# Z products in the attention drain, constants loaded early, and a two-bank GELU in quarters

## The reference

```python
x = x + tanh(g_xattn[0]) * attention(layernorm(x), ctx)   # 32 heads, 8 kv heads, rmsnorm on q and k
t = layernorm(x)[:, perm]                                 # features permuted
t = gelu(einsum('bhd,hdm->bhm', t, up))                   # 16 heads of 32 -> 128
x = x + tanh(g_ffn[0]) * einsum('bhm,hmd->bhd', t, down)[:, unperm]
p, g, v = Wp @ layernorm(x), Wg @ ctx, Wt @ ctx           # per block of 128 channels
att = sum(p * g) per group of 16 channels
y = groupnorm(Wz @ (att * v)) * gn_w + gn_b + ctx
x = x + tanh(g_xattn[1]) * y
x = x + tanh(g_ffn[1]) * experts(layernorm(x))            # one of 8 experts for each token
```

## Time and profile before

| what | value |
|---|---|
| median of 3 runs | 853.31 us (850.31 to 854.73) |
| the profiled execution | 851.44 us |
| its span in the trace | 849.7 us |
| PE busy | 770.1 us (91%) |
| ACT, DVE, POOL busy | 489.3, 484.1, 338.5 us |
| mean granted TensorE clock | 0.956 of full speed |

### The profile page before, as it was taken

The page is one execution under the profiler, slowest core; times in us unless marked ns, Lnnn a source line. Parts: engine busy times, 40 slices in busy tenths (PEclk is TensorE's granted clock), DMA queues, the critical chain, the costliest instruction groups (busy, mean ns, idle before and its releaser), DMA issues. The chain is left out here.

```text
span 849.7 us, 13807 instructions
## 1 busy us (share of the span) xinstructions
PE 770.1 (91%) x3850; PEld 605.1 (71%) x3850; DVE 484.1 (57%) x885; ACT 489.3 (58%) x1840; POOL 338.5 (40%) x639
## 2 busy tenths in 40 slices
PE   5999958999999999999999999999988888678990
PEld 3888846888888887888887888888876333255760
DVE  4775304556556555565565655655666456646773
ACT  4543217776766765766666676676552655334760
POOL 0330014443443444344353453453232455125883
PEclk9999979999999999999999999999999898867995
DMA  8435641021021021012002003000021577513436
GB/s 293 146 123 159 186 132 62 15 74 63 14 73 65 14 74 64 13 33 103 13 28 98 24 12 111 25 12 14 1 100 49 182 254 307 192 50 125 148 128 218
DMA packets 46151, 80.66 MB, mean 95 GB/s; under 512 B 5128, under 2 KB 25608, under 8 KB 42640
## 3 DMA queue, kind: packets, MB, share of 16 engines
q1 hardware_dynamic: 43536, 71.66, 24.8%
q0 software_dynamic: 2560, 8.39, 3.0%
HBM read 55.40 MB, written 24.64 MB: 94 GB/s over the span
## 5 line engine op out<-in xcount | busy, mean ns | idle before, releaser
L552 ACT ACTIVATE p_sb<-p_sb,nmax 128x128 f32<-128x128 f32 x256 | 99.7, 391 | 132.0 <-DVE nmax L698 132.0
L626 POOL TENSOR_TENSOR v_lo<-v_raw,v_hi 128x128 fp32r<-128x128 f32 x64 | 29.6, 462 | 258.2 <-ACT v_hi L590 258.2
L721 DVE TENSOR_TENSOR pT_lo<-bank,pT_hi 128x512 fp32r<-128x512 f32 x64 | 44.2, 691 | 48.9 <-ACT pT_hi L565 48.9
L763 PEld LDWEIGHTS bank<-kT,qT_sb 128*128 128x128 f32 x512 | 66.9, 191 | 7.1 <-ACT qT_sb L560 1.8
L631 POOL TENSOR_TENSOR p_sb<-p_sb,rsum 128x512 f32<-128x512 f32 x64 | 66.6, 1041 | 6.6 <-DVE rsum L717 6.6
L763 PE MATMUL bank<-kT,qT_sb 128*128 128x128 f32 x512 | 67.6, 275 | 1.4 <-ACT qT_sb L560 1.4
L597 ACT ACTIVATE q_junk<-bank 128x128 f32<-128x128 f32 x256 | 66.1, 272 | 4.2 <-PE bank L775 4.2
L689 DVE TENSOR_TENSOR oT_lo<-bank,oT_hi 128x512 fp32r<-128x512 f32 x64 | 44.0, 688 | 36.3 <-ACT oT_hi L547 36.3
L547 ACT ACTIVATE oT_hi<-bank 128x512 fp32r<-128x512 f32 x64 | 38.1, 595 | 40.2 <-PE bank L814 35.8
L392 PE MATMUL bank<-w_hi,ctx_hi 128*128 128x512 f32 x128 | 53.8, 420 | 7.6 <-DVE ctx_lo L323 7.6
L727 DVE SCALAR_TENSOR_TENSOR x_sb<-bank,tgates,x_sb 128x512 f32<-128x512 f32 x64 | 48.0, 751 | 22.0 <-PE bank L803 22.0
(11 more groups left out here) (259 smaller groups left out, 2163.8 us busy)
## 6 DMA issues: line engine op xcount, KB each, us to landing
w_raw<-in_wq_l SPq DMA_DIRECT2D x8, 1024.0 KB, 5.5
w_raw<-in_wo_l SPq DMA_DIRECT2D x8, 1024.0 KB, 4.8
exp_w<-in_exp_w_l SPq DMA_DIRECT2D x8, 1024.0 KB, 11.9
kT_scr<-kT_st SPq DMA_DIRECT2D x16, 256.0 KB, 2.3
v_scr<-v_st SPq DMA_DIRECT2D x16, 256.0 KB, 2.6
sorted_x<-ctx_nat SPq DMA_DIRECT2D x1, 3840.0 KB, 11.9
hid<-sorted_x SPq DMA_DIRECT2D x15, 256.0 KB, 2.7
sorted_y<-ctx_nat SPq DMA_DIRECT2D x15, 256.0 KB, 2.1
```

What stands on the lines that cost most here:

```text
L552: last = act.activation(p_sb[:, b % 2, h * P:(h + 1) * P], p_sb[:, b % 2, h * P:(h + 1) * P], ACT.Exp, bias=nmax[:, b % 2, h:h + 1], accum ...
L763: last = pe.matmul(s_ps[:, h * P:(h + 1) * P], qT_sb[:, b % 2, h * P:(h + 1) * P], kT[:, b * P:(b + 1) * P], start=True, stop=True)
```

## The change

1. The ten constants are issued on SP right after the load of x, and `project_kv` no longer waits for them; PE waits for them at the start of `attention` (`s.mid_ld`).
2. `s.ctx_nat` has another place in the memory, is loaded at the start of the last head group, and Z products 0 to 3 stand in the drain of `attention` (`z01`, `z2`, `z3`), each with its copy on ACT. Z products 4 to 7 stand at the start of `middle`. SP's part of `attention` now ends with a wait for the last output projection.
3. The banks are allocated in pairs. GELU reads two banks in an activation, and the `up` products cycle through three pairs. The first half of the tokens is 4 packs of 512, the second half 8 packs of 256, so there are 12 packs. The second half is scattered and loaded back in two parts (`THIRDS`), with 12 scatters in all.
4. Expert weights 0 and 1 are issued behind the stores of `xT_scr`.
5. The order of the G products, of their copies and of the later statistics changes. In `experts` the statistics of the first half end before block 4 is updated.

```diff
+QTOK = 2 * P
+HALVES = ((0, HB), (HB, B))
+THIRDS = ((0, HB), (HB, HB + 2), (HB + 2, B))
...
+            if i >= lo + 2:
+                dve.wait_ge(bn_done, i - 1)
+                dve.bn_aggr(s.mv[:, i - 2, :], s.bn[:, i - 2, :]).then_inc(mv_done, 1)
+        layernorm_var(dve, s, mv_done, hi, slice(lo, hi)).then_inc(xval_done, 1)
 
 
 def negated_shift(dve, s, cols, rstd, shift):
@@ -103,9 +106,8 @@
                                     op0=ALU.mult, op1=ALU.mult)
 
 
-def layernorm_half_var(dve, s, step, count, c=None):
-
-    cols = slice(0, B) if c is None else slice(c * HB, (c + 1) * HB)
...
+            for dst, src in ((s.up[:, :, :], d.up), (s.down[:, :], d.down), (s.perm_col[:, :], d.perm_col),
+                             (s.wt[:, :], d.wt), (s.wzT[:, :], d.wzT), (s.wgT[:, :], d.wgT), (s.wpT[:, :], d.wpT),
+                             (s.group_mean[:, :], d.group_mean), (s.gn_w[:, :], d.gn_w), (s.gn_b[:, :], d.gn_b)):
+                sp.dma_start(dst, src).then_inc(s.mid_ld, 16)
...
-            for dst, src in ((s.up[:, :, :], d.up), (s.down[:, :], d.down), (s.perm_col[:, :], d.perm_col),
-                             (s.wt[:, :], d.wt), (s.wzT[:, :], d.wzT), (s.wgT[:, :], d.wgT), (s.wpT[:, :], d.wpT),
-                             (s.group_mean[:, :], d.group_mean), (s.gn_w[:, :], d.gn_w), (s.gn_b[:, :], d.gn_b)):
-                sp.dma_start(dst, src).then_inc(mid_ld, 16)
                 sp.wait_ge(first_ld[i], 48)
             sp.wait_ge(wo_ld, 16)
-            sp.wait_ge(mid_ld, 160)
 
...
+            sp.wait_ge(q_done, 8 * G - 8)
+            sp.wait_ge(o_done, 8 * G - 8)
+            sp.dma_start(s.ctx_nat[:, :, :], d.ctx).then_inc(s.ctx_nat_ld, 16)
+            sp.wait_ge(o_done, UNITS)
...
+            def copy_z(*bs):
+                for n in bs:
+                    act.wait_ge(s.z_done, n + 1)
+                    act.activation(s.z[:, n, :], z_ps[n][:, :], ACT.Copy).then_inc(s.z_copied[1], 1)
...
+            run(act, [(oT_split, -2), (exps, 0), (copy_z01, 0), (qT_copy, 1), (pT_split, -1), (copy_z2, -1), (copy_z3, -1),
+                      (v_split, 2), (q_stats, 2), (seed_ln2, -3), (copy_xT, -6)]
...
+                if after(u, b, g, B - 3):
+                    pe.wait_ge(s.z_copied[1], 2)
...
             def transpose_x(u, b, g, odd):
                 if after(u, b, g, HB - 1):
-                    pe.wait_ge(q_scaled, UNITS)
+                    pe.wait_ge(s.z_copied[1], HB)
                     pe.wait_ge(qT_copied, UNITS)
                     pe.wait_ge(masked, UNITS)
...
+            def z01(u, b, g, odd):
+                if after(u, b, g, B - 2):
+                    pe.wait_ge(s.ctx_nat_ld, 16)
+                    pe.wait_ge(q_scaled, u + 1)
+                    pe.wait_ge(acc_done, u - 2)
+                    z_product(0)
+                    z_product(1)
+
+            def z2(u, b, g, odd):
+                if after(u, b, g, B - 2):
+                    pe.wait_ge(s.z_copied[1], 1)
+                    z_product(2)
+
+            def z3(u, b, g, odd):
+                if after(u, b, g, B - 1):
+                    pe.wait_ge(q_scaled, UNITS)
+                    z_product(3)
...
+            run(pe, [(scores, 0), (q_proj, 2), (z01, 0), (q_transpose, 1), (p_transpose, -1), (z3, -1), (o_proj, -2),
+                     (z2, -1), (values, -1), (transpose_x, -5)])
...
+        ZA, ZD = (4, 5), (6, 7)
+
+        def pack(k):
+
+            if k < KT:
+                return k, slice(0, HALF)
+            q, jt = divmod(k - KT, KT)
+            return jt, slice(HALF + q * QTOK, HALF + (q + 1) * QTOK)
+
+        def hidden(k, j):
+
+            if k < KT:
+                return hid[:, 4 * (k % 2) + 2 * j:4 * (k % 2) + 2 * j + 2, :]
+            return hid[:, 2 * (k % 4):2 * (k % 4) + 2, :].rearrange("p a (c n) -> p (a c) n", n=QTOK)[:, 2 * j:2 * j + 2, :]
+
+        def hidden_free(k):
+
+            return 0 if k < 2 else k - 1 if k < KT else (k - KT) // 2 + 3 if k < 2 * KT else k - 3
...
-            sp.wait_ge(scattered[0], 16 * KT)
-            sp.dma_start(yU[:, :, 0:HALF], d.yT_scr[0].rearrange("(k p) n -> p k n", p=P)).then_inc(yU_ld[0], 16)
-            sp.wait_ge(s.o_done, UNITS)
             for e in (0, 1):
                 sp.dma_start(s.exp_w[:, e, :, :], d.exp_w[e]).then_inc(s.exp_ld, 16)
-            sp.wait_ge(scattered[1], 16 * KT)
-            for i in range(2):
-                sp.dma_start(yU[:, :, HALF + i * 2 * P:HALF + (i + 1) * 2 * P],
-                             d.yT_scr[1][:, i * 2 * P:(i + 1) * 2 * P].rearrange("(k p) n -> p k n", p=P))\
-                    .then_inc(yU_ld[1 + i], 16)
+            for c, (lo, hi) in enumerate(THIRDS):
+                sp.wait_ge(scattered[c], 16 * KT)
+                sp.dma_start(yU[:, :, lo * P:hi * P], d.yT_scr[c].rearrange("(k p) n -> p k n", p=P))\
+                    .then_inc(yU_ld[c], 16)
             for e in (2, 3, 6, 7):
                 sp.dma_start(s.exp_w[:, e, :, :], d.exp_w[e]).then_inc(s.exp_ld, 16)
             sp.wait_ge(y_done, B)
...
+            copy_z(4)
             act.wait_ge(xval_done, 2)
...
-            for n in range(PACKS):
-                reached(act, down_done, n - 1)
-                for i in range(HG):
-                    act.wait_ge(up_done, HG * n + i + 1)
-                    act.activation(hid[:, HG * (n % 2) + i, :], up_ps[i][:, :], ACT.Gelu).then_inc(gelu_done, 1)
+            for k in range(PACKS):
+                toks = pack(k)[1]
+                reached(act, down_done, hidden_free(k))
+                for j in range(2):
+                    act.wait_ge(up_done, 4 * k + 2 * j + 2)
+                    act.activation(hidden(k, j), up_ps[(2 * k + j) % 3][:, :, 0:toks.stop - toks.start], ACT.Gelu)\
+                        .then_inc(gelu_done, 1)
             act.preload_act_table_set(LN_EXP_SET)
-            for b in range(HB, B):
-                copy_z(b)
-            for b in range(3):
+            for b in range(5):
                 copy_g(b)
             seed3(0)
+            copy_g(5)
+            copy_g(6)
             normalise3(0)
-            copy_g(3)
-            copy_g(4)
+            copy_g(7)
             seed3(1)
-            for b in (5, 6, 7):
-                copy_g(b)
             normalise3(1)
+            seed3(2)
+            normalise3(2)
             act.wait_ge(col_step, 3)
...
-            for n in range(KT):
-                scatter(n)
             pool.wait_ge(ctx_nat_ld, 16)
             pool.wait_ge(col_step, 2)
-            scale_ctx(range(HB))
-            for n in range(KT, PACKS):
-                scatter(n)
-            scale_ctx(range(HB, HB + 2))
+            for jt in range(KT):
+                scatter(0, jt)
+            scale_ctx(range(2))
+            for jt in range(KT):
+                scatter(1, jt)
+            for jt in range(KT):
+                scatter(2, jt)
+            scale_ctx(range(2, HB))
             rstd3(0)
-            scale_ctx(range(HB + 2, B))
-            add_ctx(range(3))
+            scale_ctx(range(HB, B))
+            add_ctx(range(2))
             rstd3(1)
+            add_ctx(range(2, 3))
+            rstd3(2)
             add_ctx(range(3, B))
...
             copy_xT(4)
+            copy_z(6)
             copy_xT(6)
-            copy_z(2)
-            copy_z(3)
-            for b in range(HB):
-                z_stats(b)
-
+            for k in range(PACKS):
+                jt, toks = pack(k)
+                dve.wait_ge(down_done, k + 1)
+                dve.tensor_copy(yT[:, jt, toks], yT_ps[k % 2][:, 0:toks.stop - toks.start]).then_inc(yT_copied, 1)
+                if k < B - 1:
+                    z_stats(k + 1)
...
-                if b == HB + 2:
+                if b == HB:
                     shift(0)
...
-                if b == 1:
-                    shift(1)
+                if b == 2:
+                    shift(2)
...
+            for k in range(PACKS + 1):
+                if k < PACKS:
+                    jt, toks = pack(k)
+                    pe.wait_ge(gathered[(k >= KT) * KT + jt], 16)
                     for i in range(HG):
-                        reached(pe, gelu_done, HG * (n - 1) + i + 1)
+                        if i % 2 == 0:
+                            reached(pe, gelu_done, 2 * k + i // 2 - 2)
+                            if k == 0 and i == 2:
+                                pe.wait_ge(z_copied[0], 2)
                         rows = slice(FD * i, FD * (i + 1))
-                        pe.matmul(up_ps[i][:, :], s.up[rows, jt, :], xg[rows, jt, c * HALF:(c + 1) * HALF],
-                                  start=True, stop=True).then_inc(up_done, 1)
-                if n >= 1:
-
-                    k = n - 1
-                    kt = k % KT
-                    pe.wait_ge(gelu_done, HG * (k + 1))
-                    reached(pe, yT_copied, k - 1)
+                        pe.matmul(up_ps[(2 * k + i // 2) % 3][:, i % 2, 0:toks.stop - toks.start], s.up[rows, jt, :],
```

(35 more changed lines are left out.)

142 lines of the change are left out of this document (74 added, 68 removed).

## The result

The changed kernel takes 839.46 us (median of 4 runs, 838.90 to 841.75), the kernel before 853.21 in the same session: ratio 0.9848, 95% interval 0.9815 to 0.9880. A second session gave 838.18 and 0.9835 (0.9815 to 0.9854). It is faster, as forecast, but by 13.8 and 14.9 us and not by 22. The first session's median lies 5.0 above the top of the forecast (827 to 834.5) and 0.5 above the range that takes in the rivals (824 to 839); the second session's lies inside that range. The profiled execution is 839.96, its span 838.2.

What follows compares the result with a forecast made beforehand. PE bounds the long middle of `attention`; chains of waits bound the places changed. Terms -6.5, -2.0, -11.1 and -1.5 sum to -21.1 from 851.44, so 830.3, stated as 831; forecast 827 to 834.5, with rivals 824 to 839.

Steps and rivals of the forecast that it cites:

- the rivals: Cases inside 824 to 839: gathers pay for weights (0.13), small packs not cheap (0.10), seam or drain gives less (0.10).
- GELU stage: Packs from 663.0 taking 12.0 and 9.6 with some overlap: end at 683.4 against 687.4, -4.0 in all.
- the clock behind the seam: First q projection in `attention`: shorter PE idle leaves twelve products at full speed, -2.0, bounds 0 and -2.9.
- drain -1.2: End of `attention`: Z products in PE's waits keep the clock up, -1.2, bounds +0.3 and -1.2.
- the gathers' 1.0: Second four gathers in GELU, delayed by expert weights 0 and 1 issued in front: +1.0, bounds 0 and +4.
- Constants: Seam after `project_kv`: early constants let `attention` start at 114.35, -6.5; -4.4 if something else holds the barrier.
- What starts GELU: First `up` product: a gather's landing, not DVE's z copies, ends the wait, at 661.9, -1.5.
- some overlap at the seam between the sizes: In GELU, between large and small packs: overlap assumed when adding 12.0 and 9.6 from 663.0 to 683.4.
- Rival (b): GELU: small packs not cheap, clock stays low; second half at 2.1 a pack ends 7 later, 838; chance 0.10.
- The merged activation: ACT in GELU: estimated 0.92 for an activation of two banks, 0.52 for each one before.
- Behind GELU: Last GELU to `a_col`: about 30 us, 37.7 before; `a_col` at 713.0, -12.1 for all since the drain.
- `experts`: Last stage: first-half statistics no longer wait for updates 4 and 5, -1.5, bounds 0 and -1.8.

Runs made afterwards that it cites:

- constants_alone: The kernel before with only the ten constants issued behind the load of x and PE's wait for them at the start of `attention`; 846.86 us.
- before_again: The kernel before, unchanged, run once more for a second profile; 854.30 us, ratio 1.0005.
- after_again: The changed kernel, unchanged, run once more for a second profile; 838.18 us, ratio 0.9835.
- fewer_warm: The changed kernel with 7 in place of 10 unread PE products at the start of the last stage; 839.38 us.
- weights_mid: The changed kernel with expert weights 0 and 1 issued once all eight gathers have landed; 839.45 us.
- weights_late: The changed kernel with expert weights 0 and 1 issued behind the first load of yU, as in the kernel before; 839.85 us.
- weights_last: The changed kernel with expert weights 0 and 1 issued behind all loads of y; 841.96 us.
- all_of_them: The changed kernel with 8 packs of 512, 7 unread products, `xT_scr` stores ahead of SP's wait, weights 0 and 1 after all gathers; 841.39 us.
- big_early_last: The changed kernel with 8 packs of 512, 7 unread products, `xT_scr` stores ahead of SP's wait, weights 0 and 1 behind y's loads; 835.70 us.
- early_stores_mid: The changed kernel with `xT_scr` stores ahead of SP's wait and weights 0 and 1 issued after all gathers landed; 841.20 us.
- warm_before_up: The changed kernel with four more unread PE products ahead of the first `up` product; 840.76 us.

## Why the prediction was wrong

Two steps failed. The larger is the GELU stage, its start included: forecast to end at E+29.5, where it had ended at E+32.3, it ends at E+34.7. The other is the clock behind the seam, put in as a fixed -2.0. The sum in its own terms, from the two profiled executions, up to DVE's last operation (the spans, 849.7 and 838.2, differ by 11.5):

| part | forecast | measured |
|---|---|---|
| start of `attention` | -6.5 | -7.0 |
| `attention` to E (clock -2.0, drain -1.2) | -3.2 | -0.7 |
| E to `a_col`, with the gathers' 1.0 | -9.9 | -4.9 |
| `a_col` to the end | -1.5 | +1.2 |
| sum | -21.1 | -11.4 |

The medians give 13.8; part of the second and the last line differs from profile to profile of the same code, as shown below.

**Constants: right.** 6.96 in the profile; alone 5.9 in the median.

**Clock after the seam: wrong as a fixed term.** The failed step is "an idle of 2.53 in `project_kv` and the 2.92 in the drain left later products at full speed", read from one profile. The rows of 17 profiles with the same 2.3 idle show 0 to 15 slow products, so a short idle time doesn't decide it. Nor did the 2.92 hold as a premise: in constants_alone and before_again the same wait in the drain is followed by 6.8 us at the lower level (622.6 to 629.4 and 631.0 to 637.8). `attention` took 532.4 in the mean of these 17, and 534.3 and 536.0 in the two of the kernel before, so the 2.0 and 1.2 together are not far off as a mean (1.9 to 3.6), but this is partly luck: up to the drain the mean gain is 0.5 to 0.8 and not 2.0, and the drain brings the rest. This profile had drawn 13.

**Drain: right in kind, rather too small.** From the q transposes (632.43, now 626.18) to E 22.7 and 21.4, -1.3, and the clock 1.00. Against before_again and constants_alone (24.2) it is -2.8, beyond the bound of -1.2.

**What starts GELU: wrong by 2.3**, and with it "-1.5" turned into a loss. I had the first `up` 8.0 behind E. The first gather started at 5.0 and not 4.2 (the second store's landing), and took 5.3 and not 3.8. In the kernel before the first gather landed 3.6 after its start, ahead of the stores of blocks 4 to 7 (E+6.2 and E+6.8). Now these are issued at E+5.7 and E+6.6, beside it, and the weights add about 0.3 (E+9.9 without them). That the stores are what slows it is argued from this order; no run has them apart. With the stores ahead of SP's new wait the same product comes at E+6.6: the wait that the change put ahead of them costs 3.7 here.

**GELU stage: the largest miss.** Forecast end E+29.5, measured 34.7 (34.4 in after_again, 36.0 in fewer_warm, which has this code up to there). The 5.2 are, to 0.1, 2.3 from the late start, 1.0 since the first GELU waits 2.1 for products at low clock where I had 1.1, 1.5 from the small packs (11.1 for eight, at 1.34 each and a start, in place of 9.6), and 1.2 from "some overlap at the seam between the sizes" that isn't there; the first four packs, at 11.1, were 0.9 quicker than my 12.0. Nor was the kernel before a fixed point: its second profile ended GELU at 34.1 and not 32.3. Rival (b) had the right sign: small products cost PE more than half of large ones (0.71 and 0.64 for 256 columns, 1.14 and 1.07 for 512). The merged activation went as estimated: 1.02 each, 0.92 apart; those of the small packs, with 512 columns, start 0.49 apart. The difference, 0.43 for 512 more columns, is 0.84 ns a column. The Trainium skill ("ScalarE: Activation LUTs", section "What ACT_TABLE_LOAD costs", on the ACTIVATE instruction) has 0.833 ns, and the trace agrees.

**Gathers and weights: right in size, wrong in place.** The weights, issued at 654.51, hit gathers 2 and 3 most: these landed 9.5 and 10.5 after their start, gathers 4 to 7 took 8.0 down to 6.2. Gather 4 had landed at E+20.5, ahead of pack 4 at 23.5. With the weights out of the way GELU ended 1.3 to 1.6 earlier in weights_mid, but the low clock was shorter there too (E+9.7 to 16.5, in place of 9.3 to 19.6); in weights_late and weights_last it ended no earlier, with the stalled packs. So the cost to GELU lies between 0 and 1.6 (+1.0 forecast), and `a_col` shows none of it. The price behind GELU shows once GELU is quick: 4.9 on `a_col` between all_of_them and big_early_last, with the weights beside the first scatters. The Trainium skill ("DMA: Bandwidth & Descriptors", section "Issuing engines are not separate DMA queues") states that DMAs of different issuers run on the same engines and interleave; the landings agree (scatters 2 and 3 took 7.8 and 8.5 beside the weights, the last of the four at most 2.8 without them).

**Behind GELU: right.** 30.2, forecast 29.6.

**`experts`: mis-sized.** The statistics came 1.5 earlier, as reckoned, and PE's twenty records of unread products, 10.3 us, ended 1.2 after the block they cover was ready (724.15). I had read ACT's and DVE's rows only and never asked what stood in PE's queue. From the start of the stage to the first transpose 10.26 remained of 10.62, so 0.4 came of the 1.5; the barrier took 0.3 more. By PE's last product 0.2 was left of the gain, and from there to the end, where the output is gathered, it took 19.0 in place of 18.0. Why is open; this part takes 17.6 to 19.3 in the 20 profiles. The stage as a whole takes 118.0 to 123.9, and most of that spread has a source: with ten unread products the first scatter of the sorted rows comes 29.9 to 30.7 behind the start where the clock is low for 3 to 4 us of the first 20, and 32.3 to 33.2 where it is low for 8 to 10.

**Open.** What decides how many products are slow behind the seam, and whether the low clock falls into GELU: there it came in nearly all profiles, moved when work moved, and was missing in early_stores_mid, warm_before_up and big_early_last. So the 27.3 of the last, and part of its 2.5 to 3.8 us over the changed kernel, may owe something to it; its six runs (832.49 to 837.83) are the better evidence, though they were taken in another session than the changed kernel's. The stalls in packs 9 and 10 also stay open.

## What to carry to other kernels

A saving inside a chain is worth what the next wait leaves of it: here GELU could be made 7 us shorter and nothing came out until the loads that fed the stage behind it were freed too. Before counting on an earlier result, look at the fixed work queued ahead of its reader, and at transfers issued "into free time", which move onto other transfers when the stage moves. Low-clock stretches should enter a sum as a spread, with more than one profile of the same code: what two profiles of one kernel differ by is the least that one profile can prove.

## What the runs showed that I had not expected

- The drain, with Z products in its waits, took the same 21.3 to 21.4 us in 17 profiles; without them it held a stretch at the lower clock in all three and took up to 2.8 longer. Of all the parts it gave the steadiest gain.
- The same code, with the same 2.3 us idle, gave 0 and 13 slow products and a difference of 3.3 us in `attention`.
- Removing a low-clock stretch with unread products (warm_before_up) did not shorten the stage; with the weights moved as well, the low clock came 13 us later and the stage was longer.
- In the stretches of this kernel an `up` or `down` group of 256 columns took 62% and 60% of one of 512 at the same clock.
